# Attention over pairs of heads, with queries and keys turned by DMA and the values of the pair one back at a slot's end

## The reference

```python
xn = layernorm(x)                                  # x: (32, 256, 128)
# attention, 16 heads of 64
a = xn * rsqrt(mean(xn * xn) + eps) * norm_w
q, k, v = heads(a @ Wq), heads((a @ Wkv)[:, :1024]), heads((a @ Wkv)[:, 1024:])
q, k = q / norm(q) * (q_gamma + 1) * 8, k / norm(k) * (k_gamma + 1) * 8
sim = tanh(q @ k.T / 50) * 50 / 8
att = (softmax(sim) @ v) @ Wo
# feed-forward with a low-rank update built from tokens 1 to 16
lt = xn[:, 1:17]; even, odd = lt[:, ::2], lt[:, 1::2]
m1 = (even[:, :4, :, None] * odd[:, :4, None, :]).reshape(32, 512, 128)
m2 = (even[:, 4:, :, None] * odd[:, 4:, None, :]).reshape(32, 128, 512)
h = gelu(xn @ W1.T + scale * xn @ m1.T + b1)
y = x + att + h @ W2.T + scale * h @ m2.T + b2
```

## Time and profile before

| | |
|---|---|
| median of 3 runs | 1261.8 us (1261.73 to 1263.38) |
| the profiled execution, its own time | 1261.8 us |
| its span in the trace | 1259.8 us |
| granted clock of PE, mean | 0.992 of full speed |
| busy share of PE, PEld, DVE, ACT, POOL | 93%, 77%, 82%, 86%, 73% |
| DMA traffic | 19.4 MB, 15 GB/s on the mean |

### The profile page before, as it was taken

One profiled execution on the slowest core, in us unless ns is written; L12 is line 12 of the kernel. 1 busy time (PEld: TensorE's weight loads), 2 busy tenths in 40 slices (PEclk: granted clock), 3 DMA queues, 4 the chain that ended last, 5 costly groups with the idle time before them and its releaser, 6 DMA issues.

```text
span 1259.8 us, 36165 instructions
## 1 busy us (share of the span) xinstructions
PE 1165.6 (93%) x13897; PEld 972.3 (77%) x13897; DVE 1032.2 (82%) x2153; ACT 1082.2 (86%) x2055; POOL 917.6 (73%) x1105
## 2 busy tenths in 40 slices
PE   3789999999999999999999999999999999999988
PEld 2468887778877778878778878778878778878777
DVE  6788889888889888889888889888889888888862
ACT  3589898889898889888888988888988888988885
POOL 4477777777777777877777877777777777777663
PEclk9899999999999999999999999999999999999999
DMA  4000000000000000000000000000000000000000
GB/s 132 10 11 11 14 16 7 15 15 11 15 15 7 15 15 11 15 15 7 15 15 11 14 16 7 15 15 11 14 15 7 15 15 15 10 11 11 11 6 9
DMA packets 32224, 19.41 MB, mean 15 GB/s; under 512 B 3508, under 2 KB 31288, under 8 KB 32056
## 3 DMA queue, kind: packets, MB, share of 16 engines
q1 hardware_dynamic: 32056, 17.12, 4.7%
HBM read 12.13 MB, written 4.19 MB: 13 GB/s over the span
## 4 chain that ended last, share of the span: by engine, by line
PE 42%; DVE 25%; ACT 19%; issue 11%; POOL 1%; ACTq 0%; POOLq 0%
PE ps_scores L481 8%; ACT probs L563 6%; PE ps_aux L455 5%; DVE qk L729 4%; PE ps_aux L448 4%; PE ps_aux L406 4%; PE ps_y L525 4%; DVE heads_T L738 3%; DVE sel_rows L760 3%; DVE qk L694 3%; PE ps_aux L408 3%; PE ps_aux L407 3%; ACT L596 3%; DVE norm L667 3%; ACT hid L596 3%
## 5 line engine op out<-in xcount | busy, mean ns | idle before, releaser
L905 POOL TENSOR_TENSOR probs_lo<-probs 128x512 f16<-128x512 f32 x512 | 586.3, 1150 | 235.1 <-ACT probs L563 232.9
L555 ACT ACTIVATE clamped<-ps_scores 128x512 f32<-128x512 f32 x512 | 310.3, 606 | 124.5 <-PE ps_scores L481 124.4
L563 ACT ACTIVATE probs<-clamped 128x512 f32<-128x512 f32 x512 | 324.9, 635 | 0.4
L503 PE MATMUL ps_o<-v_hi,probs 128*128 128x65 bf16 x2048 | 240.0, 195 | 4.5 <-DVE o_sb L706 2.7
L504 PE MATMUL ps_o<-v_lo,probs 128*128 128x64 bf16 x2048 | 239.2, 193 | 0.0
L505 PE MATMUL ps_o<-v_hi,probs_lo 128*128 128x65 bf16 x2048 | 238.9, 194 | 0.0
L481 PE MATMUL ps_scores<-heads_T 64*128 64x256 f16 x3072 | 212.9, 271 | 14.2 <-ACT clamped L555 14.0
L406 PE MATMUL ps_aux<-w_hi,xhT_hi 128*128 128x512 f32 x384 | 191.5, 499 | 31.9 <-DVE qk L729 21.6
L503 PEld LDWEIGHTS ps_o<-v_hi,probs 128*128 128x128 bf16 x2048 | 192.1, 99 | 30.1 <-issue 18.2
L504 PEld LDWEIGHTS ps_o<-v_lo,probs 128*128 128x128 bf16 x2048 | 189.8, 99 | 5.0
L505 PEld LDWEIGHTS ps_o<-v_hi,probs_lo 128*128 128x128 f16 x2048 | 190.2, 98 | 0.0
(11 more groups left out here) (83 smaller groups left out, 2211.2 us busy)
## 6 DMA issues: line engine op xcount, KB each, us to landing
x_in<-in_L_attn_tokens_dram SPq DMA_DIRECT2D x32, 128.0 KB, 2.3
x_res<-in_L_attn_tokens_dram SPq DMA_DIRECT2D x32, 128.0 KB, 2.3
out_dram<-y_sb SPq DMA_DIRECT2D x32, 128.0 KB, 1.9
sel_raw<-xn SPq DMA_DIRECT2D x192, 4.0 KB
qk<-in_L_attn_Wkv_dram SPq DMA_DIRECT2D x2, 512.0 KB, 5.4
qk<-in_L_attn_Wq_dram SPq DMA_DIRECT2D x1, 512.0 KB, 3.6
qk<-in_L_ffn_W_dram SPq DMA_DIRECT2D x2, 256.0 KB
hid<-in_L_attn_q_gamma_dram SPq DMA_DIRECT2D x1, 512.0 KB, 7.0
```

Source lines behind the costliest of these rows:

```text
L503: pe.matmul(full, hi[:, col], v_hi[:, par, u, h], start=(u == 0), stop=False)
L555: nc.scalar.activation(clamped[:, buf], ps_scores[:, s % SCORE_BANKS], ACT.Tanh).then_inc(clamp_done, 1)
L563: nc.scalar.activation(probs[:, buf], clamped[:, buf], ACT.Exp, bias=LIFT, scale=SOFTCLAMP * DH ** -0.5).then_inc(probs_done, 1)
L905: g.tensor_tensor(probs_lo[:, buf], probs[:, buf], probs[:, buf].bitcast(BF16)[:, 1::2], ALU.subtract).then_inc(lo_made, 1)
```

## The change

The step has 8 slots, one per pair of heads, and every engine's order is written anew.

- **Turning.** The task `qkT` is gone. ACT casts a quarter (`chunk_of`: 128x1024, the queries and keys of two pairs) of the normalised values in SBUF to fp16 (`half`), DVE subtracts it from the values for the low half (`halves`), and SP issues two DMA transposes per quarter (`turn_heads`), 128x1024 fp16 (256 KB) each, 8 per element. `halves16` holds two quarters; `half` waits for the DMAs of the quarter two before.
- **Pairs.** Tanh and exponential treat a pair at once (128x1024), and so does POOL. `clamped` has one pair, `probs` and `probs_lo` two (`RING = 2`). The scores of a pair still wait for the tanh of the pair before it.
- **Values.** The values of pair s-1 stand at the end of slot s of PE (`VALUES_LAG = 1`), behind the slot's auxiliary tasks and output products; DVE divides pair s-2 in slot s.
- **Tables.** `AUX` has 21 rows in place of 30; `xhT` and `xnT` share a bank (`xT`); ACT's, DVE's and POOL's orders are tables of their own.

The diff, cut to its core:

```diff
 AUX = [
-    (1, "k", 0, 1), (1, "k", 1, 1), (1, "q", 2, 1),
-    (2, "qkT", 4, 0), (2, "qkT", 5, 0),
...
+    (0, "k", 2, 1), (0, "k", 3, 1), (0, "oT", 0, -1),
+    (1, "v", 0, 1), (1, "v", 1, 1), (1, "oT", 1, -1),
+    (2, "low", 0, 0), (2, "v", 2, 1), (2, "v", 3, 1), (2, "oT", 2, -1),
+    (3, "xT", 0, 2), (3, "low", 1, 0), (3, "oT", 3, -1),
+    (4, "q", 0, 2), (4, "q", 1, 2),
+    (5, "hid", 0, 0), (5, "hid", 1, 0),
+    (6, "k", 0, 2), (6, "k", 1, 2),
+    (7, "q", 2, 2), (7, "q", 3, 2),
 ]
-RING = 4
-VALUES_LAG = 3
+RING = 2
+VALUES_LAG = 1
+DIVIDE_LAG = 2
+SCALAR_STEPS = [
+    [("tanh",), ("q", 3, 1), ("exp",), ("k", 2, 1), ("k", 3, 1)],
+    [("tanh",), ("half", 3, 0), ("exp",), ("oT", 0, -1), ("v", 0, 1), ("v", 1, 1)],
+    [("tanh",), ("oT", 1, -1), ("exp",), ("v", 2, 1), ("v", 3, 1)],
+    [("tanh",), ("oT", 2, -1), ("exp",), ("xT", 0, 2)],
+    [("tanh",), ("oT", 3, -1), ("exp",), ("q", 0, 2), ("q", 1, 2)],
+    [("tanh",), ("half", 0, 1), ("exp",), ("hid", 0, 0), ("hid", 1, 0)],
+    [("tanh",), ("half", 1, 1), ("exp",), ("k", 0, 2), ("k", 1, 2)],
+    [("tanh",), ("half", 2, 1), ("exp",), ("q", 2, 2)],
+]
 VECTOR_STEPS = [
...
+    [("q", 2, 1), ("divide",), ("result",), ("q", 3, 1), ("sum", 2, 1), ("sum", 3, 1), ("sum", 4, 1)],
...
+    [("sum", 6, 1), ("sum", 7, 1), ("seed",), ("divide",), ("v", 2, 1), ("v", 3, 1)],
+    [("low", 0, 0), ("halves", 3, 0), ("divide",), ("low", 1, 0)],
...
+TURN_STEPS = {3: (3, 0), 5: (0, 1), 6: (1, 1), 7: (2, 1)}
+Y_PRODUCTS = {2: 2, 3: 5, 4: 4, 5: 3, 6: 5, 7: 5}
...
+            def turn_heads(st, c, ahead):
+                b, _, _ = st.batch(ahead)
+                wait(sp, scores_done, 2 * PAIRS * (b - 1) + 4 * c + 4)
+                for half, made in enumerate((half_hi_made, half_lo_made)):
+                    sp.wait_ge(made, CHUNKS * b + c + 1)
+                    sp.dma_start(heads_T[:, half, 2 * c:2 * c + 2].rearrange("p a t j n -> p (a t j) n"),
+                                 halves16[:, c % 2, half].rearrange("p a b n -> p (a b n)"),
+                                 transpose=True).then_inc(heads_turned[c], 16)
...
             def run(st):
...
+                for s in range(PAIRS):
+                    if "attn" in st.stages:
+                        scores(st, s)
+                    for task in aux_tasks(st, s):
                         aux(st, *task)
                     if "back" in st.stages and s in Y_PRODUCTS:
                         result(st, sum(Y_PRODUCTS.get(i, 0) for i in range(s)), Y_PRODUCTS[s])
-                    late = head_of(st, s, VALUES_LAG)
+                    late = pair_of(st, s, VALUES_LAG)
                     if late:
                         values(st, *late)
...
+            def tanh(st, pair):
+                b, _, _ = st.batch(0)
+                wait(act, scores_done, 2 * PAIRS * b + 2 * pair + 2)
+                wait(act, probs_done, PAIRS * b + pair)
+                nc.scalar.activation(clamped[:].rearrange("p j n -> p (j n)"),
+                                     ps_scores[:].rearrange("p j n -> p (j n)"), ACT.Tanh).then_inc(clamp_done, 1)
...
+            def half(st, c, ahead):
+                b, par, _ = st.batch(ahead)
+                act.wait_ge(qk_normed, CHUNKS * b + c + 1)
+                wait(act, heads_turned[(c + 2) % CHUNKS], 32 * (b + c // 2))
+                nc.scalar.copy(halves16[:, c % 2, 0], chunk_of(par, c)).then_inc(half_hi_made, 1)
...
+            def halves(st, c, ahead):
+                b, par, _ = st.batch(ahead)
+                dve.wait_ge(half_hi_made, CHUNKS * b + c + 1)
+                v.tensor_tensor(halves16[:, c % 2, 1], chunk_of(par, c), halves16[:, c % 2, 0], ALU.subtract)\
+                    .then_inc(half_lo_made, 1)
```

More of the change, by code:

```diff
@@ L70 @@
-STAGE = {2: "turn", 1: "front", 0: "attn", -1: "back"}
+PER_BATCH = {"xT": 1, "q": 4, "k": 4, "v": 4, "oT": 4, "low": 2, "hid": 2}
+CHUNKS = 4
+STAGE = {3: "load", 2: "turn", 1: "front", 0: "attn", -1: "back"}
 SCORE_BANKS = 2
-RING = 4
-VALUES_LAG = 3
-VECTOR_STEPS = [
[L80 to L95, removed]
+RING = 2
@@ L322, in wait_bank, with aux_tasks, bank_of, pair_of @@
                     return
-        def aux_tasks(st, slot, kinds):
+        def aux_tasks(st, slot):
             for i, (s, kind, k, ahead) in enumerate(AUX):
-                if s == slot and kind in kinds and STAGE[ahead] in st.stages:
+                if s == slot and STAGE[ahead] in st.stages:
                     yield i, kind, k, ahead
-        def head_of(st, slot, lag):
-            ahead, head = (0, slot - lag) if slot >= lag else (-1, slot - lag + HEADS)
+        def bank_of(kind, k):
+            i = [(what, n) for _, what, n, _ in AUX].index((kind, k))
+            return ps_aux[:, i % AUX_BANKS, :]
+        def pair_of(st, slot, lag):
+            ahead, pair = (0, slot - lag) if slot >= lag else (-1, slot - lag + PAIRS)
             there = "attn" if ahead == 0 else "back"
-            return (ahead, head) if there in st.stages else None
+            return (ahead, pair) if there in st.stages else None
+        def chunk_of(par, c):
+            return qk[:, par].rearrange("p t (j n) -> p (t j) n", j=2)[:, :, c * 4 * DH:(c + 1) * 4 * DH]\
+                .rearrange("p b (a n) -> p a b n", n=P)
         def run_all(eng, run):
@@ L531, in run @@
                     pe.wait_ge(consts_loaded, 16 * 3)
-                for s in range(HEADS):
-                    if "attn" in st.stages and s % 2 == 0:
-                        scores(st, s // 2)
-                    for task in aux_tasks(st, s, PER_BATCH):
+                for s in range(PAIRS):
+                    if "attn" in st.stages:
+                        scores(st, s)
+                    for task in aux_tasks(st, s):
                         aux(st, *task)
@@ new lines, in run @@
+            def run(st):
+                for s in range(PAIRS):
+                    for what, *k in SCALAR_STEPS[s]:
+                        if what == "tanh":
+                            if "attn" in st.stages:
+                                tanh(st, s)
+                        elif what == "exp":
+                            if "attn" in st.stages:
+                                exp(st, s)
+                        elif STAGE[k[1]] in st.stages:
+                            if what == "half":
+                                half(st, *k)
+                            else:
+                                aux(st, what, *k)
```

353 lines of the change are left out of this document (161 added, 192 removed), and 6 rows, old and new, of the table AUX.

## The result

The changed kernel takes **1417.1 us** (median of 4 runs, 1410.7 to 1421.4) against 1262.5 us on the same chip: ratio 1.122 [1.1175, 1.1264], 155 us slower. The forecast was 1323, its range 1281 to 1390.

The account below looks back on a forecast made before the run. No engine bounds alone; a chain from tanh to tanh does. Its slots sum to 39.26 us per element, plus 0.3 for DVE and POOL lateness; 39.6 x 32 = 1267, plus 55.7 for the ends, gives 1323 us, range 1281 to 1390.

Parts of the forecast that it names:

- The chain: Waits from one tanh to the next, added over slots 0 to 7: 39.26 us per element, slot 2 longest at 7.23.
- The transfers: DMA transposes of the quarters: 3 us each, hidden under 4.9 us; as the bound, a rival of 2104 us, 14%.
- PE's clock falls: Rival: PE's idle gap in slot 2 lowers its clock, 2 us more per element, 1387 us; 12%.
- Both of its signs: What would show the clock rival: granted clock under 0.95 and scores over 0.83 us.
- the links of slot 3: PE's chain work behind slot 2's gap, 2.5 us, taking 1.8 times as long in the clock rival.
- An output product 0.11: PE's price per output product in us: two products 0.22 in slot 2, five 0.55 in slot 3, four 0.44 in slot 4.
- the sum: Slot lengths added from priced links, 39.26 us per element against 37.69 before; 0.3 was added on top.
- [DVE] nothing: DVE per element: 8 subtractions of 0.68 replaced by 4 of 1024 elements at 1.31, 5.2 us against 5.4.
- the ends: Start and end of the kernel outside the 32 elements, kept at 55.7 us.
- The range: 1281 to 1390 us, taking in forecast and clock rival, leaving out the transfers and cases at or under 1262.
- Rival 3: Banks read early enough, slack leaves slots 0 to 2 and ACT paces all: 35.9 us per element, 1205 us; 5%.

Follow-up runs that it names:

- run 1: Changed kernel with DVE's low-rank update moved to the head of slot 2, ahead of `v` 3: 1358.4 us.
- Run 3: Changed kernel with PE's gaps before `oT` 1 and `oT` 2 filled with 9 and 12 matmuls of constants: 1380.8 us.
- run 11: Changed kernel with PE's gaps filled by constant matmuls and the five output products of slot 3 moved to slot 6: 1512.6 us.
- run 10: Changed kernel with PE's gaps filled by constant matmuls and POOL's low half of a pair in two 512-column instructions: 1375.1 us.
- run 2: Changed kernel with the 24 output products in slots 5 to 7 in place of 2 to 7: 1465.5 us.
- run 6: Changed kernel with the next pair's scores on PE ahead of the slot's last auxiliary task: 1351.3 us.
- version 7: Changed kernel with the next pair's scores ahead of the last auxiliary task and the low-rank update at the head of slot 2: 1333.9 us.
- run 9: Run 3's kernel with two of the four squares on POOL cut from 512 to 8 columns: 1373.8 us.
- best full version: version 7 with POOL's low half of a pair in two instructions of 512 in place of one of 1024: 1253.5 us.
- run 5: Changed kernel with the previous pair's values on PE right behind the scores, ahead of auxiliary tasks and output products: 1430.8 us.
- run 13: The best full version with the third quarter's `halves` moved from slot 7 to slot 0: 1284.7 us.

## Why the prediction was wrong in size, with the chain right

Three steps failed. The fall of the clock stood as a rival beside the forecast and not as a term in it; an output product was priced at half of what it takes; and DVE's change was put at nothing by its own widths, with no look at what would run beside it. By time the first two weigh most.

- **The chain**: right. No engine bounds alone, the tanh waits for scores, slot 2 is the longest, PE stands before `oT` 2 with DVE's `w_eff` as releaser. Moving the one row of DVE's order took 3.7 us out of slot 2 (run 1). Slots 5, 6 and 7, paced by ACT's rows, came out within 0.06 us; so did the widths of 1024 (tanh 1.03 us, cast 1.05, exponential 1.07).
- **The transfers**: right, 3 us taken and 3.2 measured, hidden (scores waited 1.0 us for them in all). The 261 GB/s of the Trainium skill ("DMA: Bandwidth & Descriptors", section "Latency and other measured facts") would have given an estimate of 1.0 us; from issue to landing the trace has three times that, so the page's rate is not what a single transpose shows.
- **"PE's clock falls", kept as a rival of 12%**: it happened, beside the forecast and not in its place. Both of its signs came, a clock under 0.95 (0.934) and scores over 0.83 us (1.46). Run 3 prices it at 36 us, and at 1.40 us per element by the slots (42.62 against 41.22). The rival gave 2 us per element, 64 us, and it gave them to the links of slot 3, which did not get longer (4.87 us with and without the fill); the time went in slots 1 and 2, in 24 of 28 elements. Its factor 1.8 comes from no row; the scores measured 1.46 / 0.83 = 1.76. The start of the kernel before had a nearer row than the gap of 3.46 us. PE had stood 2.78 us before the turn of `xh`, and right behind it the clock was at its lower level (1.2 GHz), ahead of the longer gap:

```profile
38.87 0.46 PE L427 MATMUL ps_aux<-ident,xh 128*128 128x128 f32 x2 [2.78 <-DVE xh L649]
```

```profile
39.20:42.79 3.59, 0.13 (x2) 0.03 (x1) 1.49 (x3) 0.37 (x1) 1.79 (x6) 0.50 0.26 73
```

- **"An output product 0.11"**: wrong, it is 0.22 (run 11: 1.11 us for five). I read two records as two products; the counts of the groups would have told. Eleven products lie on the path of slots 2 to 4, 1.2 us by the sum, though slot 4, where other work fills in, grew by only 0.24: about 1 us per element, some 32 of the 94 us. The rival and the forecast should have been added, not weighed against each other: the forecast's own chain had the idle time behind which the clock fell. 1323 + 32 + 36 is 1391.
- **"[DVE] nothing"**: the step that failed by its reasoning. For `halves` itself it was not far off in this kernel: 1.40 us on the mean where 1.31 was taken, and 9 us in all above the subtraction that it replaces. But I kept all other rows of DVE, and `xh`, `xn` and `sel_rows`, which the change leaves alone, took 109 us more in a new order beside POOL. A part of slot 2's excess is this: PE got the update at 664.41, 5.47 us after the tanh, where the sum has 4.88; DVE had come late to `v` 2 and took `v` 2 and 3 in a row. In the changed kernel it is the smallest of the three in time (6 us by run 10 against 3, by way of DVE's own length; the rest through the clock), yet it weighs in every repair: in runs 1, 2, 6, 7 and 11 DVE took the gain back in whole or in part, and taking POOL's low halves away is worth 186 us in version 7 (in which PE's waits for them are counted too).
- What is left is some 20 us of the 94: about 6 in the ends (version 3: 1380.4 less 32 x 41.22 is 61.4, against the 55.7 taken), the rest, 0.4 us per element, in slots 0 to 3, which even with the clock held and DVE quicker (run 9) stood 0.1 to 0.25 each above the sum, the price of the products put right. I have no run on these.
- **The range**: it ended at 1390 because each case carried one fault alone. Rival 3's 1205 is 48 us under what its mechanism gave in the best full version (1253). With all but 8 columns of POOL's low halves left out the same orders took 1147, so what kept the best full version above 1205 is POOL's low halves (DVE's stand beside them, and PE's waits for them), not ACT.

## What to carry to other kernels

When a chain of waits is the forecast, price what its idle time does to the clock inside the forecast, and check a duration per operation by the count of records in its group before it is multiplied. A DVE operation beside a busy POOL is not the same operation as alone, even one that the change leaves untouched: look at who runs at the same time, and try two POOL instructions for one long one where DVE has to pass between them. A task moved "to where there is room" needs a look at the order of all engines there; four of the moves here (runs 2, 5, 11 and 13) ended in a longer wait. And a wait read in one version may be gone in the next (run 13).
